# A fused attention and expert kernel: VectorE's work order inside one token tile, and the split of the second normalization between ScalarE and VectorE

## The chip, the cores and the metric

The kernel runs on one core of one Trainium2 chip, as one program in one launch. The metric is device time in microseconds (us), the median of three runs. Engines are written as in the profile: PE is TensorE's matmul side and PEld its weight loads, DVE is VectorE, ACT is ScalarE, POOL is GpSimd, SP is SyncE, which here issues every DMA (SPq in the rows).

## The reference

Two blocks over x of shape 8 x 512 x 2048, all in float32.

```python
x = x + autocorrelation(layernorm(x), ctx, ctx)      # block 1
h = layernorm(x)                                      # block 2 from here
scores = (h @ Wq.T) @ keys.T                          # 64 experts
gate = softmax over the 16 largest scores, 0 elsewhere
z = h @ A.T                                           # 512 columns, 8 for each expert
x = x + ((z * gate) @ B.T) * 2.0
```

Block 1 correlates each head's normalized rows with the context through Fourier transforms, keeps the twelve largest lags and adds the shifted context rows. The change touches block 2 alone.

## The kernel before

Block 1 is worked off as 32 groups, written as `steps(body)`, until about 1340 us of the profiled execution. Block 2 goes over 4096 tokens in tiles of 128, so TT = 32 tiles, written as `each_tile(engine, tile_step)`: each engine has its own `tile_step(u, ...)`, and the order of the calls in it is the order of its instructions. Engines meet at semaphores only.

In step u the engines work on four tiles at once:

- PE: waits for `zg` of tile u-1 and turns it (`turn_z`, 4 transposes, L857); computes z of tile u (48 matmuls of 128x512, each product split in hi*hi + hi*lo + lo*hi, L595 to L597); scores the experts of tile u (L844); then four output banks of tile u-1, 12 matmuls each (`out_bank(q)`), with the router's 16 small matmuls of tile u+1 (`queries`, L627) between bank 0 and bank 1. Two PSUM banks serve the four outputs: `out_bank(q)` waits until `add_out(q-2)` has taken its bank. The turn of z waits for `zg`.
- DVE: `zt_low` (L1364); `turn_spread`, four 32x32 block transposes of the normalized tile u+1 (L1022); `half_statistics` of tile u+2, in two halves (L1038); `route`, the top 16 of the scores (L1329 to L1338); `tile_low(u+1, q)` for q = 0 to 3, the low part of the split input, a subtraction with both operands in SBUF (L1014); `add_out(q)`, PSUM times 2 plus the row, in place (L1359); `tile_mean` and `invert_root` of tile u+2 (L1044 to L1048, L1053); `gate_z` (L1342 to L1352), which makes `zg`; and `norm_blocks(u+2)`.
- `norm_blocks` (L1024 on DVE, L1558 on ACT) writes the normalized tile u+2 in 16 blocks of 32 partitions x 512. Block (c, b) reads the 32 rows of quarter c. ACT takes ten blocks and DVE six; `turn_spread` waits for all 16. For the first four tiles another path is used (`spread(t)` is false).
- ACT: `zt_high` (L1766), `tile_high` (L1527), the exponentials (L1772, L1774), the root and scale of tile u+2 (L1531 to L1546), then its blocks (L1565).
- POOL: for each half h of tile u+2, `add_partner` (L1899: `rows` with `cin`) and `add_input` (L1910: adds `xin`). This makes the tile that `half_statistics` reads.
- SP, in this order: `load_rows(u+2, half 1)` (L488), which first waits until all earlier stores have landed; `cin` and `xin` of half 1 (L495, L502), each after POOL has freed its buffer; `cin` and `xin` of half 0 of tile u+3; `store_half(u, 0)` (L511), after `add_out(1)`; `load_rows(u+3, half 0)`, after that store has landed; `store_half(u, 1)`, which waits for `add_out(3)`.

`cin` and `xin` are single buffers, `rows` has four.

Of the kernel before, what the change touches and what calls it, by code (L numbers as in the profile page):

```python
# [9 lines left out]
ALU = mybir.AluOpType  # L10
ACT = mybir.ActivationFunctionType
# [14 lines left out]
TT = TOKENS // P  # L26
KD = D // P
# [106 lines left out]
def build_program(nc, x, ctx, a_w, b_w, wq_w, keys, tables, out):  # L134
# [6 lines left out]
    with ExitStack() as st:  # L141
        place = [st]

        def sb(name, shape, dt=F32):
            return place[0].enter_context(nc.sbuf_tensor(name, shape, dt))
# [9 lines left out]
        def sem(name):  # L155
            return st.enter_context(nc.semaphore(name))
# [7 lines left out]
        rstd2, shift2 = sb("rstd2", [P, 1]), sb("shift2", [P, 1])  # L164
# [30 lines left out]
        rows = [sb(f"rows{n}", [P, D]) for n in range(2)]  # L195
# [51 lines left out]
        x2_added, stat2_step, root2_done, norm2_ready = (  # L247
            sem("x2_added"), sem("stat2_step"), sem("root2_done"), sem("norm2_ready"))
        xn_ready, tp_ready = sem("xn_ready"), sem("tp_ready")
        xn_part = sem("xn_part")  # L250
        tp_hi, tp_lo, tp_full = sem("tp_hi"), sem("tp_lo"), sem("tp_full")
# [38 lines left out]
        def is_step(i, n):  # L290
            return isinstance(i, int) and i == n
# [74 lines left out]
        def tp_at(t, q):  # L366
            return 4 * t + q

        def bank_of(t, q):

            return q % 2 if is_step(t, 0) else q

        def out_at(t, q):
            return 4 * t + q

        def z_bank(u):

            return out_ps[1] if is_step(u, 1) else z_ps

        def out_bank_of(u, q):  # L380

            return z_ps if is_step(u, 1) and q == 1 else out_ps[q % 2]
# [5 lines left out]
        FIRST_SPREAD = 4  # L388
        SPREAD = P // 4
        SPREAD_PARTS = 16  # L390
        BLOCKS = [(c, b) for c in range(4) for b in range(4)]
        ACT_BLOCKS, DVE_BLOCKS = BLOCKS[:10], BLOCKS[10:]

        def spread(t):
            return not (isinstance(t, int) and t < FIRST_SPREAD)

        def later_tile(u):
            return not (isinstance(u, int) and u + 2 >= TT)

        def ahead(u):  # L400

            return later_tile(u) and spread(u + 2)
# [524 lines left out]
        def _(dve):  # L927
# [81 lines left out]
            def tile_low(t, q):  # L1009

                dve.wait_ge(tp_hi, tp_at(t, q) + 1)
                part = slice(4 * q, 4 * q + 4)
                turned_x = xt_full[:, q, :, :] if spread(t) else tp_ps[bank_of(t, q)][:]
                nc.vector.tensor_tensor(xt[:, 1, part, :], turned_x, xt[:, 0, part, :].bitcast(F32),  # L1014
                                        ALU.subtract).then_inc(tp_lo, 1)
# [8 lines left out]
            def norm_blocks(t, slot, blocks):  # L1024

                dve.wait_ge(norm2_ready, 2 * t + 2)
                dve.wait_ge(q_ready, tp_at(t - 1, 3) + 1)
                by_block = xn[:].rearrange("p (k c i) -> p k c i", k=KD, c=4)
                for c, b in blocks:
                    own = slice(SPREAD * c, SPREAD * (c + 1))  # L1030
                    nc.vector.tensor_scalar(by_block[SPREAD * b:SPREAD * (b + 1), :, c, :],
                                            rows[slot][own, b * 512:(b + 1) * 512].rearrange("p (k i) -> p k i", k=KD),
                                            rstd2[own], shift2[own], ALU.mult, ALU.add).then_inc(xn_part, 1)

            def half_statistics(t, slot, h):
                dve.wait_ge(x2_added, 2 * t + h + 1)
# [13 lines left out]
            def invert_root(t):  # L1050

                dve.wait_ge(root2_done, t + 1)
                nc.vector.reciprocal(near2, near2).then_inc(stat2_step, 1)  # L1053
# [272 lines left out]
            def tile_step(u, k, r, a, b, f):  # L1326
# [13 lines left out]
                def gate_z():  # L1340
                    dve.wait_ge(gate_exp, 2 * u + 2)
                    nc.vector.reciprocal(gate_inv[:], gate_sum[:]).then_inc(gate_step, 1)  # L1342
                    dve.wait_ge(gate_step, 2 * u + 1)
                    dve.wait_ge(route_step, 5 * u + 5)
                    nc.vector.tensor_scalar(gate[:], rest[:], NEG, gate_inv[:], ALU.is_equal, ALU.mult).then_inc(gate_step, 1)
                    dve.wait_ge(gate_step, 2 * u + 2)
                    nc.vector.tensor_tensor(gate[:], gate[:], score_exp[:], ALU.mult).then_inc(gate_ready, 1)
                    dve.wait_ge(gate_ready, u + 1)
                    dve.wait_ge(z_ready, u + 1)
                    if b:  # L1350
                        dve.wait_ge(zt_ready, u)
                    nc.vector.tensor_tensor(zg[:].rearrange("p (e r) -> p e r", r=RANK),  # L1352
                                            z_bank(u)[:].rearrange("p (e r) -> p e r", r=RANK),
                                            gate[:].unsqueeze(2).broadcast_to((P, EXPERTS, RANK)), ALU.mult).then_inc(zg_ready, 1)

                def add_out(q):
                    cols = slice(q * 512, (q + 1) * 512)
                    dve.wait_ge(out_ready, out_at(u - 1, q) + 1)
                    nc.vector.scalar_tensor_tensor(rows[r][:, cols], out_bank_of(u, q)[:], SCALING, rows[r][:, cols],  # L1359
                                                   ALU.mult, ALU.add).then_inc(out_taken, 1)  # L1360

                def zt_low(t=u):
                    dve.wait_ge(zt_hi_done, t)
                    nc.vector.tensor_tensor(turned_z(t, 1), zt_ps[:], turned_z(t, 0).bitcast(F32), ALU.subtract).then_inc(zt_lo_done, 1)  # L1364
# [40 lines left out]
                    route()  # L1405
                if f:
                    tile_low(u + 1, 0)
                if is_step(u, TT - 1):
                    gate_z()
                add_out(0)  # L1410
                if f:
                    tile_low(u + 1, 1)
                if later_tile(u):
                    half_statistics(u + 2, (r + 3) % RING, 1)
                    tile_mean(u + 2)
                add_out(1)
                if later_tile(u):
                    invert_root(u + 2)
                if f:
                    tile_low(u + 1, 2)  # L1420
                    tile_low(u + 1, 3)
                if f:
                    gate_z()
                if is_step(u, TT - 1):
                    zt_low(TT)
                add_out(2)
                if ahead(u):
                    norm_blocks(u + 2, (r + 3) % RING, DVE_BLOCKS)
                add_out(3)

            each_tile(dve, tile_step)

        @block.scalar
        def _(act):
# [122 lines left out]

            def norm_blocks(t, slot, blocks):  # L1558

                act.wait_ge(norm2_ready, 2 * t + 2)  # L1560
                act.wait_ge(tp_lo, tp_at(t - 1, 3) + 1)
                by_block = xn[:].rearrange("p (k c i) -> p k c i", k=KD, c=4)
                for c, b in blocks:
                    own = slice(SPREAD * c, SPREAD * (c + 1))
                    nc.scalar.activation(by_block[SPREAD * b:SPREAD * (b + 1), :, c, :],  # L1565
                                         rows[slot][own, b * 512:(b + 1) * 512].rearrange("p (k i) -> p k i", k=KD),
                                         ACT.Identity, bias=shift2[own], scale=rstd2[own]).then_inc(xn_part, 1)

            act.wait_ge(consts_set, 2)
            nc.scalar.activation(inv_sum[:, 0:1], consts[:, 1:2], ACT.Sqrt)  # L1570
# [182 lines left out]
            def tile_step(u, k, r, a, b, f):  # L1753
# [67 lines left out]
                if ahead(u):  # L1821
                    tile_scale(u + 2)
                    norm_blocks(u + 2, (r + 3) % RING, ACT_BLOCKS)
# [228 lines left out]
```

## Time and profile before

| | us |
|---|---|
| median of 3 runs | 2121.38 |
| lowest, highest | 2120.59, 2122.97 |
| the profiled execution's own time | 2121.38 |
| its span, first to last instruction | 2119.6 |
| PE busy in the span | 2076.3 (98%) |
| DVE busy | 1881.9 (89%) |
| POOL busy | 1573.9 (74%) |
| ACT busy | 1442.8 (68%) |

The span is 1.8 us shorter than the execution's own time. A matmul's record is longer than the distance to the next one, because they are pipelined, so a gap of PE shows in the distance of two starts, and not always as idle time.

### The profile page before, as it was taken

The numbers are of one execution on the slowest core, as the hardware profiler recorded it, in microseconds if no ns is written. First come the engines' busy times: TensorE is split into PE (matmuls) and PEld (weight loads), VectorE is DVE, ScalarE is ACT, GpSimd is POOL, SyncE is SP. The second block draws the span as 40 slices with busy tenths as digits, with TensorE's granted clock in tenths as the row PEclk, the third lists the DMA queues.
The fourth block names the chain that finished last, engine by engine and source line by source line (L and its number), as shares of the span: only waits on it lengthen the run. The fifth ranks groups of instructions, "written<-read, shape, count | busy, mean of one in ns | idle before, by whom it ended". The sixth has DMA issues, their size and how long they took to land.

```text
span 2119.6 us, 28855 instructions
## 1 busy us (share of the span) xinstructions
PE 2076.3 (98%) x8472; PEld 1277.5 (60%) x8472; DVE 1881.9 (89%) x4331; ACT 1442.8 (68%) x3191; POOL 1573.9 (74%) x965
## 2 busy tenths in 40 slices
PE   5999999999999999999999999999999999999999
PEld 2455455455445445545545545688878787777877
DVE  7999999999999999999999999867878777777763
ACT  4786787787687687687776555756666666666661
POOL 6999999999999999999999998833444344343330
PEclk9999999999999999999999999999999999999999
DMA  7233243242233333323223117544554444545431
GB/s 281 91 122 105 97 137 105 85 141 101 97 125 109 105 121 113 105 105 129 85 75 119 65 45 277 205 169 169 176 182 173 173 168 173 183 166 180 168 139 60
DMA packets 110705, 287.49 MB, mean 136 GB/s; under 512 B 7169, under 2 KB 7297, under 8 KB 109569
## 3 DMA queue, kind: packets, MB, share of 16 engines
q1 hardware_dynamic: 110592, 286.19, 38.5%
q8 instruction: 46, 0.75, 0.1%
q14 instruction: 67, 0.54, 0.1%
HBM read 219.06 MB, written 67.11 MB: 135 GB/s over the span
## 4 chain that ended last, share of the span: by engine, by line
PE 33%; DVE 29%; POOL 18%; issue 8%; ACT 6%; DMA 5%; SPq 0%; DVEq 0%; POOLq 0%; ACTq 0%
POOL r_f L1865 5%; PE pair L763 4%; PE pair L769 4%; ACT xn L1565 3%; DVE prod L1068 3%; DMA cin<-out_dram 3%; DVE prod L1072 3%; PE pair L658 2%; PE evac L669 2%; DVE xt L1014 2%; PE evac L670 2%; POOL half_fold L1854 2%; PE evac L645 2%; PE lag L712 2%; POOL p_f L1865 2%
## 5 line engine op out<-in xcount | busy, mean ns | idle before, releaser
L769 PE MATMUL pair<-r_f,back 128*128 128x512 f32 x768 | 342.8, 597 | 0.5 <-DVE prod L1072 0.5
L1899 POOL TENSOR_TENSOR rows<-rows,cin 128x1024 f32<-128x1024 f32 x48 | 118.3, 2466 | 291.0 <-DMA rows<-out_dram 202.0
L1865 POOL TENSOR_TENSOR r_f<-prod 128x1024 f32<-128x1024 f32 x128 | 303.3, 2382 | 9.2 <-DVE prod L1070 7.3
L769 PEld LDWEIGHTS pair<-r_f,back 128*128 128x128 f32 x768 | 143.0, 190 | 192.8 <-issue 146.5
L1565 ACT ACTIVATE xn<-rows,shift,rstd 32x512 f32<-32x512 f32 x280 | 227.9, 814 | 7.5
L763 PE MATMUL pair<-w_sb,wts 128*128 128x512 f32 x512 | 225.1, 592 | 1.4 <-ACT w_sb L1682 0.9
L595 PE MATMUL out<-b_hi,zt_hi 128*128 128x512 f32 x492 | 199.6, 406 | 4.0 <-DVE rows L1359 4.0
L595 PE MATMUL z<-a_hi,xt 128*128 128x512 f32 x496 | 196.3, 396 | 0.0
L597 PE MATMUL z<-a_hi,xt 128*128 128x512 f32 x496 | 193.5, 390 | 0.0
L596 PE MATMUL z<-a_lo,xt 128*128 128x512 f32 x496 | 193.0, 389 | 0.0
L596 PE MATMUL out<-b_lo,zt_hi 128*128 128x512 f32 x492 | 192.5, 391 | 0.0
L597 PE MATMUL out<-b_hi,zt_lo 128*128 128x512 f32 x492 | 192.3, 391 | 0.0
L1910 POOL TENSOR_TENSOR rows<-xin,rows 128x1024 f32<-128x1024 f32 x63 | 163.5, 2595 | 8.5 <-DMA xin<-in_x_dram 3.0
L763 PEld LDWEIGHTS pair<-w_sb,wts 128*128 128x128 f32 x512 | 94.8, 190 | 108.9 <-issue 108.9
L1072 DVE TENSOR_TENSOR prod<-pair,v_cyc 128x1024 f32<-128x1024 f32 x128 | 155.5, 1215 | 0.0
L1865 POOL TENSOR_TENSOR p_f<-prod 128x1024 f32<-128x1024 f32 x64 | 151.6, 2370 | 3.9 <-DVE prod L1072 2.0
L1527 ACT ACTIVATE xt<-xn 128x512 fp32r<-128x512 f32 x124 | 69.1, 621 | 118.6 <-PE z L597 118.2
L1620 ACT ACTIVATE e<-e,neg_max 128x512 f32<-128x512 f32 x128 | 88.6, 717 | 89.4 <-DVE pick L1135 89.3
L645 PE MATMUL evac<-vf,fwd 128*128 128x512 f32 x248 | 119.7, 615 | 25.3 <-POOL vf L1925 21.3
L712 PEld LDWEIGHTS lag<-lags,p_f 128*128 128x128 f32 x1024 | 123.5, 192 | 20.7 <-issue 16.5
L1014 DVE TENSOR_TENSOR xt<-xn,xt 128x512 fp32r<-128x512 f32 x112 | 132.0, 1199 | 0.0
L712 PE MATMUL lag<-lags,p_f 128*128 128x128 f32 (+2 forms) x1024 | 129.2, 277 | 1.1 <-POOL p_f L1865 0.7
(238 smaller groups left out, 5501.5 us busy)
## 6 DMA issues: line engine op xcount, KB each, us to landing
out_dram<-att_sb SPq DMA_DIRECT2D x32, 1024.0 KB, 4.2
rows<-out_dram SPq DMA_DIRECT2D x64, 512.0 KB, 3.9
cin<-out_dram SPq DMA_DIRECT2D x63, 512.0 KB, 4.5
xin<-in_x_dram SPq DMA_DIRECT2D x63, 512.0 KB, 4.5
vf<-in_ctx_dram SPq DMA_DIRECT2D x31, 1024.0 KB, 5.1
out_dram<-rows SPq DMA_DIRECT2D x62, 512.0 KB, 2.6
xf<-in_x_dram SPq DMA_DIRECT2D x30, 1024.0 KB, 5.3
stat_in<-in_x_dram SPq DMA_DIRECT2D x27, 1024.0 KB, 5.1
```

The lines of the kernel that those rows point to most:

```text
L595: nc.tensor.matmul(out, lhs_hi, rhs_hi, start=start, stop=False)
L596: nc.tensor.matmul(out, lhs_hi, rhs_lo, start=False, stop=False)
L597: return nc.tensor.matmul(out, lhs_lo, rhs_hi, start=False, stop=stop)
L645: nc.tensor.matmul(evac_ps[n % 2][:], fwd[:, n, :], v[:, fold, :], start=True, stop=True).then_inc(evac_ready, 1)
L712: return nc.tensor.matmul(lag_ps[t % 2][:, cols], p_f[:, row, t * P:(t + 1) * P], lags[:, cols], start=True, stop=True)
L763: last = nc.tensor.matmul(to, wts[:, 4 * blk - 4 + 2 * part + h, :], w_sb[:, 2 - 2 * part + h, :], start=h == 0, stop=h == 1)
L769: return nc.tensor.matmul(pair_ps[:, bank, :], back[:, 3 * bank + n, :], r_f[:, row, :], start=n == 0, stop=n == 2)
L1014: nc.vector.tensor_tensor(xt[:, 1, part, :], turned_x, xt[:, 0, part, :].bitcast(F32), ALU.subtract).then_inc(tp_lo, 1)
L1072: op = nc.vector.tensor_tensor(slot[:, 2:4, :], s_ps, vs[:, 1:3, :], ALU.mult)
L1565: nc.scalar.activation(by_block[SPREAD * b:SPREAD * (b + 1), :, c, :], rows[slot][own, b * 512:(b + 1) * 512].rearrange("p (k i) -> p k i" ...
L1865: nc.gpsimd.tensor_tensor(dst, prod[:, slot, 0:2, :], prod[:, slot, 2:4, :], ALU.add).then_inc(add_done, 1)
L1910: nc.gpsimd.tensor_tensor(half, xin2 if second else xin[:], half, ALU.add).then_inc(x2_added, 1)
```

## The change

Three things change in block 2.

- The 16 blocks of `norm_blocks` are dealt by quarter: ACT takes quarters 0 and 1 (eight blocks) and DVE quarters 2 and 3 (eight blocks). Before it was ten and six.
- In DVE's step, `tile_low(u+1, 1)` moves ahead of `add_out(0)`; `tile_low(u+1, 2)` and `(u+1, 3)` move ahead of the second half's statistics; `add_out(3)` moves ahead of `norm_blocks`.
- In step TT-1, `gate_z` moves from in front of `add_out(0)` to behind `add_out(1)`, where the other steps have it.

ACT's two waits in `norm_blocks` stand under a condition that is true in its only call. PE, POOL and SP keep their programs.

```diff
-        BLOCKS = [(c, b) for c in range(4) for b in range(4)]
-        ACT_BLOCKS, DVE_BLOCKS = BLOCKS[:10], BLOCKS[10:]
+        ACT_BLOCKS, DVE_BLOCKS = (0, 1), (2, 3)
...
-                for c, b in blocks:
+                for c in blocks:
                     own = slice(SPREAD * c, SPREAD * (c + 1))
-                    nc.vector.tensor_scalar(...)
+                    for b in range(4):
+                        nc.vector.tensor_scalar(...)
...
                     route()
                 if f:
                     tile_low(u + 1, 0)
-                if is_step(u, TT - 1):
-                    gate_z()
+                    tile_low(u + 1, 1)
                 add_out(0)
                 if f:
-                    tile_low(u + 1, 1)
+                    tile_low(u + 1, 2)
+                    tile_low(u + 1, 3)
                 if later_tile(u):
                     half_statistics(u + 2, (r + 3) % RING, 1)
                     tile_mean(u + 2)
                 add_out(1)
                 if later_tile(u):
                     invert_root(u + 2)
-                if f:
-                    tile_low(u + 1, 2)
-                    tile_low(u + 1, 3)
-                if f:
+                if a:
                     gate_z()
                 if is_step(u, TT - 1):
                     zt_low(TT)
                 add_out(2)
+                add_out(3)
                 if ahead(u):
                     norm_blocks(u + 2, (r + 3) % RING, DVE_BLOCKS)
-                add_out(3)
```

ACT's `norm_blocks` gets the same two loops. (`f`: u+1 < TT; `a`: u < TT.)

## Rows read from the trace of the kernel before

**Rows 1.** The page: busy time of each engine.

```profile
PE 2076.3 (98%) x8472; PEld 1277.5 (60%) x8472; DVE 1881.9 (89%) x4331; ACT 1442.8 (68%) x3191; POOL 1573.9 (74%) x965
```

**Rows 2.** Timeline of PE, turns of z: start, length, instruction, count.

```profile
1431.48 0.38 PE L857 MATMUL zt<-ident,zg 128*128 128x128 f32 x2
...
1816.17 0.38 PE L857 MATMUL zt<-ident,zg 128*128 128x128 f32 x2
...
2057.93 0.27 PE L857 MATMUL zt<-ident,zg 128*128 128x128 f32 x1
...
2081.66 0.27 PE L857 MATMUL zt<-ident,zg 128*128 128x128 f32 x1
...
2098.70 0.60 PE L857 MATMUL zt<-ident,zg 128*128 128x128 f32 x4
```

**Rows 3.** Timeline of PE, end of bank 2 and start of bank 3, tile 1816.17.

```profile
1836.96 0.39 PE L597 MATMUL out<-b_hi,zt_lo 128*128 128x512 f32 x1
1837.66 0.50 PE L595 MATMUL out<-b_hi,zt_hi 128*128 128x512 f32 x1 [0.31 <-DVE rows L1359]
```

**Rows 4.** Timeline of DVE in the tile that starts at 1816.17.

```profile
1816.59 3.43 DVE L1031 TENSOR_SCALAR xn<-rows,rstd,shift 32x512 f32<-32x512 f32 x6
1820.05 0.69 DVE L1359 SCALAR_TENSOR_TENSOR rows<-out,rows 128x512 f32<-128x512 f32 x1
1823.79 0.69 DVE L1364 TENSOR_TENSOR zt_lo<-zt,zt_hi 128x512 fp32r<-128x512 f32 x1 [3.06 <-ACT zt_hi L1766]
...
1829.33 0.68 DVE L1014 TENSOR_TENSOR xt<-xn,xt 128x512 fp32r<-128x512 f32 x1
1830.71 0.69 DVE L1359 SCALAR_TENSOR_TENSOR rows<-out,rows 128x512 f32<-128x512 f32 x1 [0.70 <-PE out L597]
1831.32 1.49 DVE L1014 TENSOR_TENSOR xt<-xn,xt 128x512 fp32r<-128x512 f32 x1
1835.10 1.29 DVE L1038 BATCH_NORM_STATS2 bn_x<-rows 128x6 f32<-128x512 f32 x2 [2.28 <-POOL rows L1910]
...
1836.92 0.68 DVE L1359 SCALAR_TENSOR_TENSOR rows<-out,rows 128x512 f32<-128x512 f32 x1
...
1837.59 1.27 DVE L1014 TENSOR_TENSOR xt<-xn,xt 128x512 fp32r<-128x512 f32 x2
...
1839.61 0.69 DVE L1352 TENSOR_TENSOR zg<-z,gate 128x512 f32<-128x512 f32 x1
```

**Rows 5.** Timeline of POOL, same tile.

```profile
1820.00 2.40 POOL L1899 TENSOR_TENSOR rows<-rows,cin 128x1024 f32<-128x1024 f32 x1 [9.71 <-DMA rows<-out_dram]
...
1829.83 2.43 POOL L1899 TENSOR_TENSOR rows<-rows,cin 128x1024 f32<-128x1024 f32 x1 [4.95 <-DMA cin<-out_dram]
1832.34 2.72 POOL L1910 TENSOR_TENSOR rows<-xin,rows 128x1024 f32<-128x1024 f32 x1
```

**Rows 6.** Timeline of SP's issues, same tile.

```profile
1823.72 0.33 SPq L488 DMA_DIRECT2D rows<-out_dram  x1
1824.31 0.33 SPq L495 DMA_DIRECT2D cin<-out_dram  x1
```

**Rows 7.** Time from issue to landing, 1500 to 2050 us: first `cin` (L495), then `xin` (L502).

```profile
DMA to landing us min/median/max: 3.6/4.4/5.5
...
DMA to landing us min/median/max: 3.1/4.9/6.2
```

**Rows 8.** Timeline of ACT, its blocks of the next tile.

```profile
1839.11 7.54 ACT L1565 ACTIVATE xn<-rows,shift,rstd 32x512 f32<-32x512 f32 x9
```

**Rows 9.** Timeline, a DVE block beside a POOL addition.

```profile
1891.99 0.55 DVE L1031 TENSOR_SCALAR xn<-rows,rstd,shift 32x512 f32<-32x512 f32 x1
...
1892.37 2.43 POOL L1899 TENSOR_TENSOR rows<-cin,rows 128x1024 f32<-128x1024 f32 x1 [9.55 <-DMA rows<-out_dram]
```

**Rows 10.** Timeline of DVE in step TT-1.

```profile
2081.86 0.69 DVE L1359 SCALAR_TENSOR_TENSOR rows<-out,rows 128x512 f32<-128x512 f32 x1 [1.60 <-PE out L597]
...
2098.91 0.69 DVE L1359 SCALAR_TENSOR_TENSOR rows<-out,rows 128x512 f32<-128x512 f32 x1 [1.90 <-PE out L597]
```

More of the change, by code:

```diff
@@ L1028, in norm_blocks @@
                 by_block = xn[:].rearrange("p (k c i) -> p k c i", k=KD, c=4)
-                for c, b in blocks:
+                for c in blocks:
                     own = slice(SPREAD * c, SPREAD * (c + 1))
-                    nc.vector.tensor_scalar(by_block[SPREAD * b:SPREAD * (b + 1), :, c, :],
-                                            rows[slot][own, b * 512:(b + 1) * 512].rearrange("p (k i) -> p k i", k=KD),
-                                            rstd2[own], shift2[own], ALU.mult, ALU.add).then_inc(xn_part, 1)
+                    for b in range(4):
+                        nc.vector.tensor_scalar(by_block[SPREAD * b:SPREAD * (b + 1), :, c, :],
+                                                rows[slot][own, b * 512:(b + 1) * 512].rearrange("p (k i) -> p k i", k=KD),
+                                                rstd2[own], shift2[own], ALU.mult, ALU.add).then_inc(xn_part, 1)
             def half_statistics(t, slot, h):
@@ L1558, in norm_blocks @@
             def norm_blocks(t, slot, blocks):
-                act.wait_ge(norm2_ready, 2 * t + 2)
-                act.wait_ge(tp_lo, tp_at(t - 1, 3) + 1)
+                if blocks[0] == 0:
+                    act.wait_ge(norm2_ready, 2 * t + 2)
+                    act.wait_ge(tp_lo, tp_at(t - 1, 3) + 1)
                 by_block = xn[:].rearrange("p (k c i) -> p k c i", k=KD, c=4)
-                for c, b in blocks:
+                for c in blocks:
                     own = slice(SPREAD * c, SPREAD * (c + 1))
-                    nc.scalar.activation(by_block[SPREAD * b:SPREAD * (b + 1), :, c, :],
-                                         rows[slot][own, b * 512:(b + 1) * 512].rearrange("p (k i) -> p k i", k=KD),
-                                         ACT.Identity, bias=shift2[own], scale=rstd2[own]).then_inc(xn_part, 1)
+                    for b in range(4):
+                        nc.scalar.activation(by_block[SPREAD * b:SPREAD * (b + 1), :, c, :],
+                                             rows[slot][own, b * 512:(b + 1) * 512].rearrange("p (k i) -> p k i", k=KD),
+                                             ACT.Identity, bias=shift2[own], scale=rstd2[own]).then_inc(xn_part, 1)
             act.wait_ge(consts_set, 2)
```

## The prediction

> **What bounds the kernel now.** I read the page's busy times first. PE is busy for 98% of the span [rows 1], so a gain can only come from the places where PE is held, and block 2's tiles are where the change sits. Next I read PE's timeline at the turns of z, one for each tile [rows 2]. From 1431.48 to 2057.93 us lie 26 tiles in 626.45 us, 24.09 us each. The tile from 2057.93 to 2081.66 takes 23.73 us, and nothing holds PE in it. I take 23.74 us as what PE's own work needs, so the 26 tiles hold 626.45 - 26 x 23.74 = 9.2 us of waiting. That is all this change can win in them: 0.43% of the time.
>
> Where PE waits is seen at the seam of bank 2 and bank 3 [rows 3]. Below, times of a tile count from its turn of z; for the tile shown that is 1816.17. Matmuls follow each other every 0.23 us, so bank 3 could start at 1837.19, which is 21.0; it starts at 21.49, released by DVE's L1359. That is `add_out(1)`, which ends at 1837.60 or 21.43 [rows 4]. So a tile costs nothing extra as long as `add_out(1)` ends by about 21.0, and the tile grows by whatever it is later.
>
> Why is it late? Going back in DVE's timeline [rows 4]: the second half's statistics start at 18.93, after an idle time that POOL's L1910 ended, and `add_out(1)` ends 2.50 us after that start. POOL's addition runs 1832.34 to 1835.06 and the one before it from 1829.83, released by the DMA into `cin` [rows 5]. SP issued that DMA at 1824.31, behind the `rows` load of 1823.72 [rows 6]. That load waits for the store of the previous tile's second half, and the store for `add_out(3)`, which DVE reaches only after six blocks of `norm_blocks`: it ends at 1820.74, 4.57, and the load is issued 2.98 us later. It is a ring: `add_out(3)`, store, load, POOL, statistics, `add_out(1)`, bank 3.
>
> A second effect matters for the moved subtractions. `tile_low` takes 0.68 us alone (1829.33). The next one starts at 1831.32 and ends at 1832.81, 0.55 us after POOL's L1899 ended (1829.83 + 2.43 = 1832.26) [rows 4, 5]. One that is issued during an addition is held until 0.55 us after its end; two can be held in a row.
>
> **The change, part by part.** All durations are of one execution, 2121.38 us, which is also the median.
>
> *`add_out(3)` ahead of `norm_blocks`.* Bank 3 is ready 0.20 us after the next turn of z, as in step TT-1, where no block stands ahead (2081.86 against 2081.66) [rows 2, 10]. So `add_out(3)` runs 0.20 to 0.89, not 3.88 to 4.57. SP's load follows 2.98 us behind: issued at 3.9, not 7.55. `cin` of half 1 is then no longer behind it, but waits for POOL's first addition of half 0. That starts at 3.83 in the row; I take 4.0, since the store now lands in the same time as the load of `rows`. It ends at 6.4, so `cin` is issued at 6.5, not 8.14. It landed within 5.52 us in the row, with three loads under way; alone, loads take from 3.6 us up [rows 5 to 7]. I take 4.1: POOL's half 1 starts at 10.6, not 13.66. `xin` of half 1 waits for the second addition of half 0, which ends at 4.0 + 2.5 + 2.4 = 8.9. Its shortest landing is 3.1 us and its median 4.9 [rows 7]; nothing is issued beside it now, so I take 3.8, 12.7. POOL's last addition runs 13.0 to 15.4, or, if a subtraction gets in first, 13.5 to 16.2 (2.72 us, as in the row) [rows 5]. Before it ended at 18.89.
>
> *The three subtractions ahead of `add_out`.* `tile_low(0)` is ready at 13.16 as before, since `route` waits for PE's scores. Held by POOL's last addition it ends at 15.4 + 0.55 = 15.95. Then follow, each 0.6 us after the one before (two free subtractions take 1.27 us, with an overlap) [rows 4], `tile_low(1)` 16.55, `add_out(0)` 17.15, `tile_low(2)` and `(3)` 18.35. Bank 2 wants `add_out(0)` by 18.3 (bank 3's 21.02 less twelve matmuls of 0.227), so PE isn't held there. The statistics start at 18.3 and `add_out(1)` ends 2.5 us later, at 20.8. In the other order, with `tile_low(0)` first and `tile_low(1)` held until 16.75, it ends at 21.0. Both are at or below 21.0: the wait is gone, or nearly. The point at which it comes back is a last addition that ends after 16.2. What the row can't show is how long these loads take alone; at `xin`'s median of 4.9 the addition would end at 16.5 and each tile would lose 0.3 us. I keep that for the range.
>
> `gate_z` no longer has two subtractions ahead of it. `zg` ended 2.70 us after `add_out(1)` (1840.30 against 1837.60), now 1.27 us less, about 1.5: at 22.3, with the turn at 23.74. It covers itself; without the move it would be ready at 23.5, close.
>
> *The blocks.* ACT's come one each 0.84 us (7.54 / 9) [rows 8], DVE's one each 0.57 (3.43 / 6) [rows 4]. ACT starts 1.5 us after `add_out(1)`: eight end at 20.8 + 1.5 + 6.7 = 29.0, which is 5.3 of the next tile. DVE's eight run from 0.92 to 5.5. Before, DVE then stood idle 3.06 us for ACT's `zt_hi` and started `zt_low` at 7.62; now it can at about 6.0 [rows 4]. The two blocks more on DVE cost 1.14 us and lie in that idle time. If that cover were gone they would still only delay `zt_low` to its old place.
>
> One risk is that DVE's blocks now run to 5.5 and POOL's additions start at 4.0. A block that lay 0.17 us beside an addition took 0.55 us like all others [rows 9], but it had started first, which says little. For a clean sum I take no contention. The rate speaks for this: 0.57 us for 512 columns is nearly what the statistics (1.29 us for two of that width) and the two-input subtractions (1.27 us for two) take [rows 4], so nothing is done at double rate.
> The Trainium skill (SBUF — State Buffer, Who interferes with whom) says that VectorE and GpSimd share one port pair, an exclusive lock held for a whole instruction, and that VectorE needs it with two SBUF inputs or in a two-port mode, which `tensor_scalar` may enter. The held `tile_low` agrees (1.49 us against 0.68). For the blocks the row shows neither the fast mode nor a real test, and the rule gives the third rival below.
>
> *`gate_z` in step TT-1.* Before, it hid in front of `add_out(0)`, and the turn of z came straight after bank 1, at 2098.70 [rows 2]. Now it is behind `add_out(1)`, which runs 2098.91 to 2099.60 [rows 10], and its four instructions take 1.44 us (from 1838.86, when the subtractions end, to 1840.30) [rows 4]. So `zg` is there at 2101.0 and the turn starts 0.06 us later, 2101.1: PE stands still for 2.4 us. Bank 2 and bank 3 are queued behind the turn, so nothing hides it, and the end of the kernel follows. Bounds: 2.1 to 2.8.
>
> **Sum.** 2121.4 - 9.2 (all waits of 26 tiles) + 0.4 (my allowance for tiles in which the addition ends a little late) + 2.4 (last turn) = 2115.0 us, 0.30% faster.
>
> **Rivals.**
> 1. *The transfers collide.* The store now meets the load of `rows`, and all moves up by less than I say. If POOL's last addition ends at 16.6 instead of 15.4 to 16.2, each tile waits 0.35: 2121.4 - 9.2 + 26 x 0.35 + 2.4 = 2123.7. Landing times from 3.1 to 6.2 us speak for it, the spreading out of four issues against it. Its range is 2118 to 2125.
> 2. *POOL's additions don't move, and the subtractions queue behind them* (slower). If `rows` and `cin` land as before, `tile_low(1)` ends at 16.6, `tile_low(2)`, issued at 17.3, is held until 18.89 + 0.55, the fourth ends at 20.0, and `add_out(1)` at 22.5: 1.5 us late in each tile, 2121.4 - 9.2 + 26 x 1.5 + 2.4 = 2154. It decides as soon as that addition ends after 16.6. Against it stands the chain through SP, whose waits all name `add_out(3)` or POOL.
> 3. *The blocks need POOL's port.* Six blocks are done at 4.3; the seventh waits for 6.4 and ends at 7.0, the eighth for the second addition, 8.9, and ends at 9.5. `zt_low` and the transposes come some 3 us later than planned, `tile_low(0)` perhaps at 15.5, with POOL done: `add_out(1)` ends at 15.5 + 0.6 x 5 + 2.5 = 21.0 to 21.3. That is 26 x 0.2 = 5 us given back: 2120.
>    This is the case that the skill's two-port rule would give (SBUF — State Buffer, Who interferes with whom); no row here shows a block held.
> 4. *No effect in the tiles*, the tail alone: 2123.8. It would need the ring to run through something else than `add_out(3)`.
>
> **Chances.** Forecast 0.62; rival 1 0.17; rival 2 0.09; rival 3 0.07; rival 4 0.05. The measurement of this kernel can tell about 0.2%, 4.2 us, from no change. Faster (below 2117.1): the forecast and a little of 1 and 3, 0.65. Slower (above 2125.6): rival 2 and the upper end of 1, 0.13. The same: 0.22. The range goes from the full gain with the smallest tail cost and 1 us of scatter, 2121.4 - 9.2 + 2.1 - 1.0 = 2113.3, to the middle of rivals 1, 3 and 4: 2113 to 2122. The forecast's own range is 2113 to 2117.
>
> **What the changed profile would show.** PE: turns of z every 23.7 to 23.8 us and no idle time before bank 3. DVE: `add_out(3)` at 0.2 in each tile; the first `tile_low` up to 2.9 us long; `add_out(1)` ending at 20.5 to 21.0; 3 or 4 us idle before `route`. POOL: half 1 from about 10.6. SP: `store_half` h = 1 at 1.1. Last tile: about 2.4 us idle on PE before the last turn of z, released by DVE's L1352. The prediction is wrong if POOL's last addition ends after 16.6, if L1031 shows lengths of over 1 us, or if the tail costs more than one chain of `gate_z`.

## The result, and the profile after

The changed kernel takes 2144.88 us (median of 3 runs, 2141.78 to 2147.70), against 2121.38 us before. The ratio is 1.0109, with a 95% interval from 1.0085 to 1.0134: it is 1.1% slower, where 0.3% faster was forecast. The profiled execution took 2148.67 us, its span is 2146.9 us, 27.3 us longer than before.

Where these 27.3 us lie is read off the turns of z. Timeline of PE in the kernel after:

```profile
1431.08 0.38 PE L856 MATMUL zt<-ident,zg 128*128 128x128 f32 x2
...
2081.22 0.27 PE L856 MATMUL zt<-ident,zg 128*128 128x128 f32 x1
...
2104.96 0.27 PE L856 MATMUL zt<-ident,zg 128*128 128x128 f32 x1
```

The same 26 tiles that took 626.45 us [rows 2] take 650.14 us, 25.0 us each instead of 24.1: 23.7 us. The next turn follows after 23.74 us as before. The last one comes 19.35 us later (at 2124.31, shown further down), not 17.04: 2.3 us. From there to the end it is 22.6 us, not 20.9: 1.7 us. Less 0.4 us with which the stretch starts earlier, that is all of it.

The waits of the 26 tiles name the place. The view of waits, kernel after, 1431 to 2081 us (total us, times, longest):

```profile
PEld out L594 <- DVE rows L1359: 38.4, 47, 1.7
...
PE out L594 <- DVE rows L1359: 19.2, 37, 1.3
```

PE still waits for `add_out`, more than before: the same two rows have 14.3 and 4.0 us in the kernel before. It now waits at two seams. By the distances of its starts it loses 0.36 us a tile ahead of bank 2 and 0.83 ahead of bank 3; before, it was 0 and 0.34. One tile shows how. Timeline of DVE, kernel after, in the tile whose turn of z is at 1857.12:

```profile
1857.32 0.69 DVE L1359 SCALAR_TENSOR_TENSOR rows<-out,rows 128x512 f32<-128x512 f32 x1 [1.02 <-PE out L596]
1858.04 8.49 DVE L1031 TENSOR_SCALAR xn<-rows,rstd,shift 32x512 f32<-32x512 f32 x8
1866.56 0.69 DVE L1364 TENSOR_TENSOR zt_lo<-zt,zt_hi 128x512 fp32r<-128x512 f32 x1
...
1870.74 0.21 DVE L1329 COPY scores<-score_sums 128x64 f32<-128x64 f32 x1
...
1872.10 3.15 DVE L1013 TENSOR_TENSOR xt<-xn,xt 128x512 fp32r<-128x512 f32 x2
1875.17 0.68 DVE L1359 SCALAR_TENSOR_TENSOR rows<-out,rows 128x512 f32<-128x512 f32 x1
1875.77 1.28 DVE L1013 TENSOR_TENSOR xt<-xn,xt 128x512 fp32r<-128x512 f32 x2
1876.98 1.27 DVE L1038 BATCH_NORM_STATS2 bn_x<-rows 128x6 f32<-128x512 f32 x2
...
1878.79 0.68 DVE L1359 SCALAR_TENSOR_TENSOR rows<-out,rows 128x512 f32<-128x512 f32 x1
```

Timeline of POOL, same tile:

```profile
1861.31 2.40 POOL L1898 TENSOR_TENSOR rows<-rows,cin 128x1024 f32<-128x1024 f32 x1 [12.46 <-DMA rows<-out_dram]
1863.78 2.46 POOL L1909 TENSOR_TENSOR rows<-xin,rows 128x1024 f32<-128x1024 f32 x1
1869.23 2.41 POOL L1898 TENSOR_TENSOR rows<-rows,cin 128x1024 f32<-128x1024 f32 x1 [2.99 <-DMA cin<-out_dram]
1871.72 2.38 POOL L1909 TENSOR_TENSOR rows<-xin,rows 128x1024 f32<-128x1024 f32 x1
```

Timeline of SP's issues, same tile:

```profile
1858.19 0.36 SPq L510 DMA_DIRECT2D out_dram<-rows  x1
1862.62 0.33 SPq L487 DMA_DIRECT2D rows<-out_dram  x1
1863.90 0.33 SPq L494 DMA_DIRECT2D cin<-out_dram  x1
1866.27 0.33 SPq L501 DMA_DIRECT2D xin<-in_x_dram  x1
```

And timeline of PE, the first matmuls of bank 2 and of bank 3:

```profile
1875.91 0.50 PE L594 MATMUL out<-b_hi,zt_hi 128*128 128x512 f32 x1 [0.34 <-DVE rows L1359]
...
1879.52 0.50 PE L594 MATMUL out<-b_hi,zt_hi 128*128 128x512 f32 x1 [0.58 <-DVE rows L1359]
```

Read against [rows 3 to 6], with times counted from the turn of z:

- `add_out(3)` starts at 0.20, the store goes at 1.07 and the `rows` load at 5.50. It was 7.55 before, and 3.9 had been worked out: about half of the gain in this place is there.
- The eight blocks take 8.49 us, not 4.6. They end at 9.41. They lie beside both additions of POOL (4.19 to 9.12). `route` starts at 13.62 instead of 11.8.
- POOL's last addition ends at 16.98. It was 18.89, and 15.4 to 16.2 had been worked out.
- The first subtraction is held by it and the second waits in line behind the first (3.15 us for the two), then come `add_out(0)`, two more subtractions and the statistics. `add_out(1)` ends at 22.35, which is 5.37 us after POOL's end; in the row of before it was 21.43, 2.54 us after it.
- Bank 2 starts at 18.79 and bank 3 at 22.40; unheld they would start at 18.3 and 21.0, and in the row of before bank 3 started at 21.49.

So in these two tiles POOL is done 1.9 us earlier and `add_out(1)` is 0.9 us later. Two things could stand behind that: DVE's blocks, held beside POOL, and the new place of the subtractions.

### The profile page after: what moved, and what is told of

Its sections match the earlier page's. It is cut to its first block, busy times and chain, and to the rows that moved or that the text cites. A ratio compares the mean times of both kernels' runs of the same rounds, so it can differ in the third digit from the quotient of the medians.

```text
span 2146.9 us, 28855 instructions
## 1 busy us (share of the span) xinstructions
PE 2086.6 (97%) x8472; PEld 1277.8 (60%) x8472; DVE 1997.1 (93%) x4387; ACT 1397.4 (65%) x3135; POOL 1567.5 (73%) x965
## 4 chain that ended last, share of the span: by engine, by line
DVE 42%; PE 28%; POOL 17%; issue 10%; ACT 2%; DMA 1%; DVEq 0%; SPq 0%; POOLq 0%; ACTq 0%
DVE xn L1031 8%; POOL r_f L1864 6%; DVE prod L1068 4%; PE pair L762 3%; DVE bn_x L1038 3%; DVE xt L1013 3%; DVE xn L1021 3%; DVE prod L1072 3%; PE out L594 3%; POOL half_fold L1853 3%; PE pair L768 2%; PE out L596 2%; PE out L595 2%; POOL p_f L1864 2%; DVE pick L1135 2%
## 5 line engine op out<-in xcount | busy, mean ns | idle before, releaser
L1031 DVE TENSOR_SCALAR xn<-rows,rstd,shift 32x512 f32<-32x512 f32 x224 | 222.3, 993 | 7.5
L594 PE MATMUL out<-b_hi,zt_hi 128*128 128x512 f32 x492 | 203.7, 414 | 19.4 <-DVE rows L1359 19.2
L1564 ACT ACTIVATE xn<-rows,shift,rstd 32x512 f32<-32x512 f32 x224 | 182.4, 814 | 6.0
L1909 POOL TENSOR_TENSOR rows<-xin,rows 128x1024 f32<-128x1024 f32 x63 | 156.8, 2489 | 9.4 <-DMA xin<-in_x_dram 4.1
L1359 DVE SCALAR_TENSOR_TENSOR rows<-out,rows 128x512 f32<-128x512 f32 x127 | 86.9, 684 | 54.4 <-PE out L596 54.4
```

The lines of the kernel that those rows point to most:

```text
L594: nc.tensor.matmul(out, lhs_hi, rhs_hi, start=start, stop=False)
L1909: nc.gpsimd.tensor_tensor(half, xin2 if second else xin[:], half, ALU.add).then_inc(x2_added, 1)
```

## Experiments

"A" is the end of `add_out(1)` and "E" the end of POOL's last addition, counted from the tile's turn of z. Both are means over 25 tiles, the 26 of the result section without the first. A tile's length is the time between two turns of z, as the mean of these 25 tiles and the one behind them, which nothing holds (it takes 23.7 us, and 24.0 in experiment 2). By this count the changed kernel has 24.95 us a tile, not the 25.0 of the section above.

**1. Ten and six blocks again, new order kept.**

```diff
-        ACT_BLOCKS, DVE_BLOCKS = (0, 1), (2, 3)
+        BLOCKS = [(c, b) for c in range(4) for b in range(4)]
+        ACT_BLOCKS, DVE_BLOCKS = BLOCKS[:10], BLOCKS[10:]
```

The loops of `norm_blocks` go back with it.

> The changed kernel, with the blocks dealt ten to ACT and six to DVE again; the order of DVE's work stays the new one. Theory A (the blocks are what costs: DVE's eight run into POOL's additions and are held, 9.41 us instead of 5.5 as their end): six blocks run from 0.92 to about 4.4, at most one is held, route starts at 11.7 again instead of 13.6, and the tiles come back to 23.74 us; with the last turn's 4 us that is about 2116 us. Theory B (the order of the subtractions costs: POOL's last addition ends at 16.5 to 17 in the changed kernel, because the store and the loads now meet, and two subtractions are held by it ahead of add_out(0)): route comes at 11.7, but add_out(1) still ends near 21.8, tiles of 24.5 us, about 2136 us. If neither is right it stays at 2145.

2133.54 us, ratio 1.0055 (1.0038 to 1.0073), tiles of 24.31 us. `route` starts on time again, `zt_low` ends at 8.3 instead of 10.0. E is 16.76, the same as in the changed kernel (16.75), and A 21.38 instead of 22.07. Theory B comes closest (24.5 us, 2136 us): giving back the blocks recovers 0.64 us of the 1.21 us that a tile loses against 23.74, not all of it.

**2. The deal of the blocks alone.** The kernel before, `BLOCKS[:8], BLOCKS[8:]`.

> The kernel before, with only the deal of the blocks changed to eight and eight. Theory A (a block that is issued during an addition of POOL is held until it ends): the seventh and eighth block, due at 3.9 and 4.4 us of the tile, are held by POOL's first two additions and end at 6.8 and 9.4; add_out(3) stands behind them, so the store, the loads and POOL's second half slip by more than 4 us, and tiles take 27 us or more: above 2190 us. Theory B (the blocks aren't held, only the order of the subtractions and the landing times count): the two more blocks put add_out(3) and all behind it 1.1 us later, tiles of 25.2 us, about 2150 us.

2207.62 us, ratio 1.0395 (1.0378 to 1.0412), tiles of 27.42 us: theory A's price and not B's. The mean hides two kinds of tile, which take turns from the fifth on. In long ones (30.0 to 31.7 us) the last blocks are held by POOL, `add_out(3)` stands behind them and ends at 9.5 to 9.8 us, and POOL's last addition ends at 22.7 to 23.9. In the short ones between them (23.7 to 25.2 us) `add_out(3)` ends at 3.5 to 6.4. Blocks are held, then. In this kernel they hold what the ring hangs on; in the changed one `add_out(3)` is ahead of them.

Not all of the 86 us are the ring's. Towards the end of each long tile, where PE waits for `add_out(1)`, the granted clock falls to 0.5 for 3.4 or 6.8 us. From `add_out(1)` to the next turn of z it takes 3.8 us in the mean instead of 2.9, so some 0.8 us a tile, 22 us in all, are the clock's. The view by windows (stretch, length, busy of PE, PEld, DVE, ACT and POOL, granted clock, here 0.93, DMA share, GB/s):

```profile
1560.00:1660.00 100.00, 89.98 (x464) 72.18 (x463) 77.50 (x163) 50.01 (x83) 34.25 (x14) 0.93 0.41 146
```

**3. `add_out(3)` alone.**

```diff
                 add_out(2)
+                add_out(3)
                 if ahead(u):
                     norm_blocks(u + 2, (r + 3) % RING, DVE_BLOCKS)
-                add_out(3)
```

> The kernel before, with only add_out(3) moved ahead of norm_blocks (six blocks on DVE, subtractions where they were). Theories A and B agree here: the six blocks run from 0.9 to 4.4 and meet POOL's first addition by 0.5 us at most, the store is issued near 1.1, POOL's last addition ends near 16.6 instead of 17.9 to 18.9, and add_out(1), 2.5 to 3.0 us behind it, ends at 19.1 to 19.6, before bank 3 wants it at 21.0. Tiles of 23.74 us, 2121.4 - 9.2 = 2112 us. Rival: the early store meets the load of rows, takes 4 us or more instead of 2.65, and gives all of it back: 2121 us.

2111.91 us in five runs, ratio 0.9956 (0.9942 to 0.9970): 0.44% faster than before, tiles of 23.74 us. Timeline of PE, first and last turn of the 26 tiles:

```profile
1454.92 0.27 PE L857 MATMUL zt<-ident,zg 128*128 128x128 f32 x1
...
2072.16 0.38 PE L857 MATMUL zt<-ident,zg 128*128 128x128 f32 x2
```

617.24 us: every wait for `add_out` in these tiles is gone. In this kernel too DVE's blocks are held (the longest 2.78 us, the six of them end at 8.3 in most tiles), since POOL now starts at 2.1 to 3.1. It costs nothing. The expectation had been that they would hardly meet.

One tile of this kernel (turn of z at 1834.76) is needed further down. Timelines of SP (store of half 1, `rows`, `cin`) and of POOL:

```profile
1835.83 0.36 SPq L511 DMA_DIRECT2D out_dram<-rows  x1
1838.69 0.33 SPq L488 DMA_DIRECT2D rows<-out_dram  x1
1839.84 0.33 SPq L495 DMA_DIRECT2D cin<-out_dram  x1
...
1845.32 2.41 POOL L1899 TENSOR_TENSOR rows<-rows,cin 128x1024 f32<-128x1024 f32 x1 [3.15 <-DMA cin<-out_dram]
```

**4. The subtractions alone.**

```diff
                     tile_low(u + 1, 0)
+                    tile_low(u + 1, 1)
                 ...
                 add_out(0)
                 if f:
-                    tile_low(u + 1, 1)
+                    tile_low(u + 1, 2)
+                    tile_low(u + 1, 3)
```

> The kernel before, with only the three subtractions moved. Theory B (they wait in line behind POOL ahead of add_out): POOL's additions stay where they are, add_out(1) ends near 22.5 and bank 2 is held as well, tiles of 25.2 to 25.8 us, 2150 to 2165 us. Theory A (only the blocks are held to any effect): POOL's second half comes at the same time and the subtractions cost nothing, tiles as before, 2121 us.

2142.13 us, ratio 1.0093 (1.0077 to 1.0109), tiles of 24.89 us. A is 22.01 and E 17.25, 4.8 us apart; before they were 2.8 apart. The loss is theory B's in kind, but smaller than its 25.2 to 25.8 us a tile; it had left POOL's additions where they were, and E came down from 18.4 with the change.

**5. The changed kernel with the subtractions put back.** The reverse of the diff in 4; eight and eight blocks, early `add_out(3)` and the moved last `gate_z` stay.

> The changed kernel, with the three subtractions put back where they were; the eight and eight blocks, the early add_out(3) and the last gate_z stay. Theory B in its present form (two effects add up: the new order puts add_out(1) 4.8 us behind the end of POOL's last addition instead of 2.5 to 3.0, and the held blocks make route 1.9 us late, which costs one subtraction more): the blocks are still held until 9.4 us of the tile, but add_out(1) ends at 20.3 to 21.2 and tiles take 23.74 to 23.9 us: 2116 to 2120 us. Theory A (held blocks alone cost the 1.2 us in each tile): 2145 us as now.

2114.44 us, ratio 0.9966 (0.9953 to 0.9978). One move of three short instructions is worth 2144.88 - 2114.44 = 30 us. Timeline of PE in this kernel, two turns of z in a row:

```profile
1977.22 0.27 PE L856 MATMUL zt<-ident,zg 128*128 128x128 f32 x1
...
2000.95 0.38 PE L856 MATMUL zt<-ident,zg 128*128 128x128 f32 x2
```

Timeline of POOL, its last addition of that tile:

```profile
1989.74 2.40 POOL L1910 TENSOR_TENSOR rows<-xin,rows 128x1024 f32<-128x1024 f32 x1
```

Timeline of DVE, same tile:

```profile
1978.14 8.50 DVE L1031 TENSOR_SCALAR xn<-rows,rstd,shift 32x512 f32<-32x512 f32 x8
1986.67 0.69 DVE L1364 TENSOR_TENSOR zt_lo<-zt,zt_hi 128x512 fp32r<-128x512 f32 x1
...
1992.21 0.68 DVE L1013 TENSOR_TENSOR xt<-xn,xt 128x512 fp32r<-128x512 f32 x1
1992.81 0.68 DVE L1359 SCALAR_TENSOR_TENSOR rows<-out,rows 128x512 f32<-128x512 f32 x1
1993.41 0.68 DVE L1013 TENSOR_TENSOR xt<-xn,xt 128x512 fp32r<-128x512 f32 x1
1994.01 1.28 DVE L1038 BATCH_NORM_STATS2 bn_x<-rows 128x6 f32<-128x512 f32 x2
...
1995.83 0.68 DVE L1359 SCALAR_TENSOR_TENSOR rows<-out,rows 128x512 f32<-128x512 f32 x1
```

The blocks take 8.50 us, as long as in the changed kernel, and `route` is as late. But POOL's last addition ends at 14.92, `add_out(1)` at 19.29, and PE never waits. Theory A falls for this kernel: where `add_out(3)` is ahead of the blocks and the subtractions are in their old places, held blocks cost a tile nothing. (With `add_out(3)` behind them they do cost, see 2.)

**6. Blocks eight and eight with the early `add_out(3)`,** without the other two moves.

> The kernel before with the eight and eight blocks and the early add_out(3); the subtractions and the last gate_z where they were. Theory B: the blocks are held by POOL until about 9.4 us of the tile and still cost nothing, tiles of 23.74 us, 2112 us, the same as with the early add_out(3) alone. Theory A (held blocks cost by themselves): above 2114 us, tiles of 23.8 us or more.

2112.94 us in five runs, ratio 0.9959 (0.9946 to 0.9973), tiles of 23.74 us, blocks held until 9.4. It can't be told from experiment 3.

**7. `add_out(0)` ahead of the second subtraction,** in the changed kernel; all three still ahead of the statistics.

> The changed kernel with add_out(0) ahead of the second subtraction; the other two stay ahead of the statistics. If the loss is bank 2 waiting for add_out(0), it goes away and tiles take about 24.3 us, 2128 us. Theory B: what counts is how many subtractions stand between the end of POOL's last addition and add_out(1), and that is the same number; tiles of 24.9 to 25.0 us, 2143 us.

2142.81 us, ratio 1.0098 (1.0082 to 1.0113), tiles of 24.75 us, one of 27.7 among them, in which the clock fell. PE's wait ahead of bank 2 is gone (0 instead of 0.36 us a tile), and the one ahead of bank 3 has grown by about as much (1.02 instead of 0.83). So bank 2's wait isn't what makes the tile long. The count of subtractions that end between E and A fits it: 3.9 a tile here and in the changed kernel, with A 5.3 us behind E in both; 2.9 in experiment 1 and 3 in experiment 4, with 4.6 and 4.8 us.

**8. The disputed cost by itself.** Each form ran eight times alone and eight times beside three additions of POOL. An excerpt of the program:

```python
for beside in (0, 1):
    if beside:
        dve.wait_ge(done_p, 3 * f)
    for n in range(OPS):
        form(n).then_inc(done_d, 1)
    dve.wait_ge(done_d, OPS * (2 * f + beside + 1))
```

> The disputed cost by itself: of the computation nothing is left; nine forms of a DVE instruction are each run eight times alone and eight times beside three additions of POOL (128x1024, about 2.4 us each). The forms: the kernel's block; the block with constants instead of the two per-partition operands; a block within one quarter, contiguous; 128 partitions wide, with operands and with constants; the block read from PSUM; a subtraction with two SBUF inputs; the 32x32 transposes; the statistics. If held means a second SBUF input, only the subtraction is held; the block reads one tensor, and its operands. If tensor_scalar from SBUF to SBUF is what is held, the first five forms are and the block from PSUM isn't. If it is the per-partition operands in SBUF, the forms with constants run free.

The trace by line, in the order of the forms; after the count stand the shortest, the median and the longest length in ns. The median is that of a free one.

```profile
L165 DVE TENSOR_SCALAR xn<-rows,rstd,shift x16: 533/545/2449, 12.2 to 26.6; 32x512 f32<-32x512 f32 x16
...
L171 DVE TENSOR_SCALAR xn<-rows x16: 415/421/2450, 27.2 to 40.0; 32x512 f32<-32x512 f32 x16
...
L177 DVE TENSOR_SCALAR wide<-rows,rstd,shift x16: 531/544/2659, 40.5 to 53.9; 32x512 f32<-32x512 f32 x16
...
L182 DVE TENSOR_SCALAR wide<-rows,rstd,shift x16: 534/542/2665, 54.5 to 67.6; 128x512 f32<-128x512 f32 x16
...
L187 DVE TENSOR_SCALAR wide<-rows x16: 414/421/2562, 68.2 to 79.8; 128x512 f32<-128x512 f32 x16
...
L192 DVE TENSOR_SCALAR xn<-bank,rstd,shift x16: 804/814/821, 80.3 to 92.9; 32x512 f32<-32x512 f32 x16
...
L198 DVE TENSOR_TENSOR wide<-rows,other x16: 677/678/2828, 93.8 to 109.5; 128x512 f32<-128x512 f32 x16
...
L203 DVE STREAM_TRANSPOSE wide<-rows x16: 665/668/711, 110.2 to 119.3; 128x512 f32<-128x512 f32 x16
...
L207 DVE BATCH_NORM_STATS2 stats<-rows x16: 675/676/695, 120.0 to 129.0; 128x6 f32<-128x512 f32 x16
```

Every `tensor_scalar` from SBUF to SBUF is held, up to 2.67 us, whatever its partitions, layout and operands; so is the subtraction of two SBUF tensors, up to 2.83. The block read from PSUM, the transposes and the statistics are free. DVE and POOL take turns: in each of these five forms and the subtraction three instructions are held, one for each addition. The same block takes 0.545 us from SBUF and 0.814 from PSUM. Whether that is a higher rate or a smaller fixed part can't be told from these runs, which have one size only.
The Trainium skill (SBUF — State Buffer, Who interferes with whom) says that `tensor_scalar`, which can enter a two-port mode, and an instruction with two SBUF inputs need the port pair shared with GpSimd, and that one with at most one SBUF input outside those modes doesn't. The trace agrees: the six forms of the first two kinds are held, and the other three (821 ns at the longest from PSUM, 711 and 695) are not.

**9. The last `gate_z` alone,** the kernel before with `if f:` made `if a:` around the later call and the early one taken out.

> The kernel before, with only the last step's gate_z moved behind add_out(1). The plain sum: PE stands still for 2.3 to 2.4 us ahead of the last turn of z, and the end is that much later, 2123.8 us. Theory C (the standstill also costs clock): in the changed kernel the matmuls after that turn follow each other every 0.43 us instead of 0.23 for some 4 us, so the end comes 4.0 us later, 2125.4 us, and the granted clock of that stretch is below 1.

2123.93 us in ten runs, against 2122.14 in its session, ratio 1.0012 (1.0002 to 1.0021). In its profile the last turn comes 19.36 us after the one before, not 17.05, and the end 22.57 us behind it, not 20.89. So the profiled execution shows theory C, and the median lies at the plain sum. Three of the ten runs have a mean clock of 1.000, and a fall of 3.4 us would have taken 0.0008 off it, so in these three it didn't fall.

**10. Eleven matmuls in place of the standstill,** added to 9.

```diff
                         if is_step(u, TT - 1) and q == 1:
+                            for _ in range(11):
+                                nc.tensor.matmul(tp_ps[0][:]..., xt[:, 0, 0, :], a_hi[:, 0, :], start=True, stop=True)
                             turn_z(TT)
```

> As the run with only the last gate_z moved, with 11 matmuls of 128x512 into an unused PSUM bank ahead of the last turn of z, which fill the 2.3 us in which PE would stand still (work added, the output unchanged). Theory C: no matmul is then at half speed and the end comes 2.3 to 2.7 us later than before instead of 4.0: 2124 us. If the clock has nothing to do with the standstill, it stays at 4.0 or more: 2125.4 us or above.

2124.42 us in ten runs, ratio 1.0008 (0.9998 to 1.0018). The last turn comes after 19.60 us, and the end 20.85 us behind it. By profile the slow matmuls are gone; the median can't tell 9 and 10 apart, so in times this is inconclusive.

**11 and 12. A second look at each.**

> A second look at the kernel before with only the last gate_z moved. Theory C: PE stands still for 2.3 us ahead of the last turn of z, and behind it some ten matmuls follow each other every 0.43 us, in most executions and not in all: a granted clock of 0.5 for 3 us within the last 25 us, ahead of the very end.

> A second look at the kernel with 11 matmuls in place of that standstill. Theory C: every matmul behind the last turn of z follows the one before in 0.23 us, and the granted clock falls only behind the last matmul.

2127.06 us and 2126.45 us, one execution each. The profiles repeat: behind the standstill, matmuls 0.43 us apart and the end after 22.52 us; with the filler none, and 20.89 us. The two times differ by less than the profiles say, because of something that lies before block 2. In seven profiled executions (1, 6, 7 and 9 to 12) the granted clock also fell at 64 to 66 us, for 3.4 or 6.8 us, and their 26 tiles start at 1432.2 to 1432.5 or at 1433.8 to 1434.3 us. In those of the changed kernel, of the kernel before and of 3, 4 and 5 it didn't, and they start at 1431.1 to 1431.5 (in 2 neither, its tiles being longer already: 1432.9). A scatter of up to 3 us in the times has this source and not the change.

This is what such a place looks like in the changed kernel. Timeline of PE in the changed kernel:

```profile
2121.79 0.39 PE L596 MATMUL out<-b_hi,zt_lo 128*128 128x512 f32 x1
2124.31 0.66 PE L856 MATMUL zt<-ident,zg 128*128 128x128 f32 x4 [2.13 <-DVE zg L1352]
...
2126.57 0.63 PE L594 MATMUL out<-b_hi,zt_hi 128*128 128x512 f32 x1
2126.99 0.63 PE L595 MATMUL out<-b_lo,zt_hi 128*128 128x512 f32 x1
```

The view by windows of the changed kernel (columns as in experiment 2):

```profile
2125.70:2129.10 3.40, 3.40 (x9) 2.65 (x8) 0.62 (x1) 0.00 (x0) 0.00 (x0) 0.51 0.00 0
```

The same stretch in the kernel of experiment 10, by windows:

```profile
2105.00:2108.40 3.40, 3.40 (x17) 2.82 (x16) 1.23 (x2) 0.00 (x0) 0.00 (x0) 1.00 0.00 0
```

PE stands still for 2.1 us, and in the 3.4 us from 1.4 us behind the turn the granted clock is 0.51: the lower of the two levels, 1.2 GHz. Nine matmuls fit in instead of seventeen, which costs 1.7 us. Six profiled executions have this standstill, of 2.13 us in each. In four of them the clock fell behind it for 3.4 us, from 0.1 to 1.4 us after the turn on (the changed kernel, 1, 9 and 11); in two it didn't (5 and 7). It didn't with the filler, in either of two, nor at this place in the five without the standstill (before, 2, 3, 4 and 6). What decides between the four and the two isn't settled.

## Why the prediction was wrong

All effects in one table (26 tiles, by profile; medians of each session, before 2120.4 to 2122.5 us):

| blocks 8 and 8 | early `add_out(3)` | subtractions ahead | last gate moved | tile, us | median, us |
|---|---|---|---|---|---|
| | | | | 24.09 | 2121.4 |
| x | | | | 27.42 | 2207.6 |
| | x | | | 23.74 | 2111.9 |
| | | x | | 24.89 | 2142.1 |
| | | | x | 24.10 | 2123.9 |
| x | x | | | 23.74 | 2112.9 |
| x | x | | x | 23.74 | 2114.4 |
| | x | x | x | 24.31 | 2133.5 |
| x | x | x | x | 24.95 | 2144.9 |

**What bounds the kernel: right.** PE's own 23.74 us a tile, the 9.2 us of waiting at bank 3, and the ring through `add_out(3)`, store, loads, POOL and statistics. Moving `add_out(3)` alone wins these 9.2 us: 2111.9 us.

**The step that failed: "Both are at or below 21.0: the wait is gone, or nearly."** It rests on POOL's last addition ending at 15.4 to 16.2. Measured, E is 16.75, and A 22.07 instead of 20.8 to 21.0. The term that was too small is the landing of `cin` of half 1: "I take 4.1" from issue to landing, because nothing else was to be under way. It took 4.98 us in the mean, as long as before (5.01). It was issued at 6.76, for which I had 6.5, and so POOL's half 1 started at 11.8, not 10.6. That is 1.2 of the 1.35 us.

The loads do collide, as rival 1 says, but not through the store that it names. The store of half 1 did take 4.2 us instead of 2.65, and the `rows` load behind it went at 5.4, not 3.9; yet this load had landed at 9.1, well before `cin` at 11.7. In experiment 3 the store took 2.7 us and the `rows` load went at 3.9, and `cin` still took 5.2 us: in the tile shown there POOL starts 5.5 us after its issue. What is common to these cases is that `rows` and then `xin` are under way beside it; `cin` of half 0, issued with no other load under way, took 3.7 us. That the other loads are the cause isn't tested.

**The ring had to be walked once more.** With `add_out(3)` out of the way it closes through `add_out(1)` itself: A, the store of half 0 (2.65 us), the `rows` load of half 0 (4.0 us), POOL's half 0 from 4.1, `cin` of half 1, POOL's half 1, E, and A again. From A of one tile to E of the next it takes 19.4 to 19.7 us in all six kernels with the early `add_out(3)` (after: 16.75 - (22.07 - 24.95) = 19.6; experiment 3: 15.12 - (19.39 - 23.74) = 19.5). So a tile can't be shorter than this plus what lies between E and A. After: 19.6 + 5.3 = 24.9; experiment 1: 19.7 + 4.6 = 24.3. The forecast had 5.4 between E and A (15.4 to 20.8). With 19.6 that is 25.0, which is what came; only by a way from A to E of 18.3 us (15.4 + 2.9) did it come out at PE's 23.74.

**Rival 1's price needed `route` on time.** It took 0.35 us a tile for an end at 16.6, with `tile_low(0)` done before POOL's last addition. In experiment 1 that is so, and the price is about right: 4.6 us between E and A, tiles 0.6 us above 23.74 with E at 16.76. In the changed kernel `route` starts at 13.6, late by the held blocks, and one subtraction more falls behind E: a held one, a second behind it, `add_out(0)`, two more and 2.5 us, 5.3 us in all, and tiles 1.2 us above 23.74.

Rival 2 had the mechanism, subtractions that queue behind POOL and delay the statistics, and tied it to additions that don't move at all; they moved, by 1.7 us, and the order ate it and more. In the old order two of the subtractions lie behind `add_out(1)`, the way around is shorter than PE's own 23.74 us, and the ring runs down to E at 15.1 to 15.2 and A at 19.4 to 19.5 (experiments 3, 5 and 6). The forecast treated the two edits as helping each other; by the table the second undoes the first.

**The blocks.** "For a clean sum I take no contention" was wrong, and rival 3 right in its mechanism: they are held, until 9.4. My reason, the rate, was a bad reading. The block's 0.54 us holds 0.12 us for the two per-partition operands; without them the 512 columns take 0.42, well below the 0.68 of the statistics, and read from PSUM the same block takes 0.81. The price was misplaced. With `add_out(3)` ahead of them, held blocks cost nothing with the old order of the subtractions and 0.64 us a tile with the new, because they make `route` late and so put one more subtraction behind POOL.

**The last `gate_z`.** The last turn was forecast 2.4 us later, bounds 2.1 to 2.8; it came 2.30 us later. The fall of the clock behind it, 1.7 us more in most of the profiled executions, was not foreseen.

**`gate_z` and `zt_low`.** As worked out, `zg` comes 1.5 us after `add_out(1)` and holds nobody, and `zt_low`, late by 3.4 us against the plan, still ends before bank 0 needs it at 11.5.

The three signs that the prediction named for being wrong all came: POOL's last addition ends after 16.6, L1031 shows lengths of up to 2.8 us, and the tail costs 4.0 us, more than one chain of `gate_z`.

The best version seen is experiment 3. Its tiles are at PE's own time, and nothing in these runs shows a way below that with these matmuls.

## What to carry to other kernels

Where an engine's late result feeds its own next input through other engines and transfers, count what stands between the last input's arrival and the result: each short instruction moved in there is paid in full and comes around again. Test such edits one at a time, since one that wins (here 9 us) can hide under one that loses (30 us). An estimate that ends at the threshold itself is a forecast of a wait, not of its absence.

## What the runs showed of the hardware

- A VectorE `tensor_scalar` from SBUF to SBUF in float32 that is issued beside a running GpSimd addition (128x1024) is held: 2.4 to 2.8 us instead of 0.54. A subtraction of two SBUF tensors is held too, 2.8 us instead of 0.68. From PSUM (0.81 us), as a transpose (0.67) or as statistics (0.68) an instruction isn't.
- The two per-partition operands cost 0.12 us: 0.542 us against 0.421 with constants, at 128 partitions and, within 3 ns, at 32.
- After a standstill of TensorE of 2.1 us the granted clock fell to the lower level for 3.4 us, from 0.1 to 1.4 us after its next matmul on, in four executions of six; at that place without the standstill in none of seven.
- A store of 512 KB that meets a load landed after 3.9 to 5.3 us instead of 2.65. A load of 512 KB issued with no other under way (`cin` of half 0) landed after 3.7 us, one issued behind one load and ahead of another (`cin` of half 1) after 5.0.
